# Four slots of one bank for the narrow score rows, and their products issued two steps ahead

## What is computed

```python
b, s, d = x.shape                                  # 2, 1024, 512
qkv = jnp.einsum('bsd,od->bso', x, w_project)
q, k, v = ...                                      # 16 heads of 32
att = jnp.einsum('bhqd,bhkd->bhqk', q, k) / math.sqrt(HEAD_DIM)
att = jnp.where(causal[None, None, :, :], jnp.float32(-1000000000.0), att)
att = jax.nn.softmax(att, axis=-1)
out = jnp.einsum('bhqk,bhkd->bhqd', att, v)
...
h = h + _L0_attn_ref(_layernorm(h, axis=-1), ...)
h = h + _L0_ffn_ref(_layernorm(h, axis=-1), ...)
```

## Time and profile before

| | us |
|---|---|
| median of three runs | 1048.05 (1047.25 to 1049.69) |
| the profiled execution | 1050.3 |
| its span, first to last instruction | 1048.5 |
| TensorE busy | 942.9 (90%) |
| VectorE busy | 667.6 (64%) |
| ScalarE busy | 599.9 (57%) |
| GpSimd busy | 322.1 (31%) |
| mean granted TensorE clock, share of full | 0.964 |

### The profile page before, as it was taken

One profiled execution on the slowest core, in us unless ns is written; L12 is line 12 of the kernel. 1 busy time (PEld: TensorE's weight loads), 2 busy tenths in 40 slices (PEclk: granted clock), 3 DMA queues, 4 the chain that ended last, 5 costly groups with the idle time before them and its releaser, 6 DMA issues.

```text
span 1048.5 us, 21182 instructions
## 1 busy us (share of the span) xinstructions
PE 942.9 (90%) x6811; PEld 687.2 (66%) x6811; DVE 667.6 (64%) x1746; ACT 599.9 (57%) x1304; POOL 322.1 (31%) x320
## 2 busy tenths in 40 slices
PE   6668599999999999999998899899889899989992
PEld 5324458677686868677685687777766566656661
DVE  8885257565666757566676676668756466656660
ACT  7222177677777777776778622211157677766770
POOL 2286120110202020110202036433233575457642
PEclk9689799999999999999999999899889999999997
DMA  6133733260533334150435111431449577747543
GB/s 213 39 97 95 169 82 82 60 134 1 115 79 82 82 72 93 47 131 17 90 77 200 42 71 61 184 148 51 163 151 335 131 135 166 241 83 135 101 71 41
DMA packets 44574, 114.39 MB, mean 109 GB/s; under 512 B 9332, under 2 KB 11380, under 8 KB 42162
## 3 DMA queue, kind: packets, MB, share of 16 engines
q1 hardware_dynamic: 32146, 87.14, 28.2%
q0 software_dynamic: 12320, 25.90, 13.7%
HBM read 53.03 MB, written 25.17 MB: 75 GB/s over the span
## 4 chain that ended last, share of the span: by engine, by line
PE 54%; DMA 20%; issue 9%; DVE 8%; POOL 4%; ACT 3%; POOLq 1%; DVEq 0%; ACTq 0%
DMA out<-xnT,slot_out 20%; PE psum L527 11%; PE psum L497 8%; PE psum L517 7%; PE psum L540 7%; PE psum L502 5%; PE psum L1259 5%; PE psum L1243 3%; PE psum L1341 2%; PE psum L543 2%; POOL hot_all L1479 1%; DVE oh_lo L1554 1%; ACT probsT L594 1%; DVE oh_hi L1552 1%; PE psum L1284 1%
## 5 line engine op out<-in xcount | busy, mean ns | idle before, releaser
L651 DVE CUSTOM_DVE_ANT_0 psum<-psum,mask_row 128x128 f32<-128x128 f32 (+7 forms) x256 | 194.2, 763 | 58.7 <-PE psum L517 56.3
L609 ACT ACTIVATE probs<-psum,nmax 128x128 f32<-128x128 f32 (+7 forms) x256 | 190.7, 745 | 48.2 <-DVE nmax L651 42.4
L527 PE MATMUL psum<-ident,probs 128*128 128x128 f32 x1152 | 172.6, 275 | 4.7 <-ACT probsT L594 3.3
L517 PE MATMUL psum<-k_stack,q_stack 128*128 128x512 f32 (+2 forms) x384 | 154.9, 458 | 18.7 <-ACT probs L609 9.1
L527 PEld LDWEIGHTS psum<-ident,probs 128*128 128x128 f32 x1152 | 136.1, 140 | 37.1 <-issue 18.6
L594 ACT COPY probsT<-psum 128x512 f32<-128x512 f32 (+3 forms) x256 | 129.3, 505 | 37.7 <-PE psum L527 32.9
L497 PE MATMUL psum<-xnT,w_unit 128*128 128x512 f32 x256 | 131.3, 602 | 0.2 <-ACT full L472 0.2
L873 POOL DMA_INDIRECT out<-xnT,slot_out x47 | 94.3, 2005 | 112.5 <-DMA out<-xnT,slot_out 94.5
L444 POOL CAST part_hi<-full 128x512 fp32r<-128x512 f32 x32 | 19.6, 613 | 351.5 <-ACT full L472 246.8
L517 PEld LDWEIGHTS psum<-k_stack,q_stack 128*128 128x128 f32 x384 | 68.5, 201 | 64.0 <-ACT probs L609 41.0
L1392 PE MATMUL psum<-w_dn,gated_T 128*128 x188 | 88.6, 593 | 1.0 <-ACT gated_T L926 1.0
(11 more groups left out here) (238 smaller groups left out, 1845.8 us busy)
## 6 DMA issues: line engine op xcount, KB each, us to landing
w_gu<-in_wgu SPq DMA_DIRECT2D x16, 1024.0 KB, 6.9
q_stack<-part_hi SPq DMA_DIRECT2D x64, 128.0 KB, 2.4
q_stack<-part_lo SPq DMA_DIRECT2D x64, 128.0 KB, 2.4
k_stack<-part_hi SPq DMA_DIRECT2D x64, 128.0 KB, 2.4
k_stack<-part_lo SPq DMA_DIRECT2D x64, 128.0 KB, 2.4
w_dn<-in_wd SPq DMA_DIRECT2D x16, 512.0 KB, 8.8
out<-acc SPq DMA_DIRECT2D x17, 256.0 KB, 2.0
hot_all<-xn SPq DMA_DIRECT2D x4, 1024.0 KB, 8.0
```

What stands on the lines that cost most here:

```text
L517: mm = pe.matmul(dst[:, c0:c1], qs, k_stack[b][:, h, c0:c1], start=True, stop=True)
L527: mm = pe.transpose(bank(4 + m % 2)[:, (j - 4 * k) * P:(j - 4 * k + 1) * P], probs[n % PSLOTS][:, j * P:(j + 1) * P], ident[:, :])
L609: act.activation(probs[n % PSLOTS][:, 0:(i + 1) * P], bank(2 * (n % 2), 2)[:, 0:(i + 1) * P], ACT.Exp, bias=nmax[:, n % 4:n % 4 + 1], scal ...
L651: dve.tensor_tensor_reduce(out=row, in0=row, in1=mask_row[:, (QT - 1 - i) * P:QT * P], scale=1.0, scalar=3.0e38, op0=ALU.add, op1=ALU.min, ...
```

## The change

Steps 0 to 15 get four slots of one bank (`score_bank`: bank n % 4), and steps 16 to 31 keep the two slots of two banks. TensorE issues the narrow score products one step earlier: step n of its loop issues that of n + 2 while this is below 16, the last step of a unit (and the start of the program's attention) issues those of steps 0 and 1 of the next, step 14 issues none, and from step 15 on it is n + 1 as before. The waits follow the slots: a narrow product waits for the exponential of step n - 4 (steps 0 to 3: for those of the unit before that had the banks), step 16 for that of step 13, the last owner of its two banks, and the others as before. VectorE's minimum and ScalarE's exponential read the new place. No instruction is added or removed.

```diff
+        NARROW = STEPS // 2
+
+        def score_bank(n):
+            return bank(n % 4) if n < NARROW else bank(2 * (n % 2), 2)
...
             def scores(u, b, n):
                 i, h = n // GH, n % GH
 
-                pe.wait_ge(s_E, HEAD + u * STEPS + n - 1)
-                dst = bank(2 * (n % 2), 2)
+                if n < 2:
+                    pe.wait_ge(s_E, HEAD + u * STEPS - 1)
+                elif n < 4:
+                    pe.wait_ge(s_E, HEAD + u * STEPS)
+                elif n < NARROW:
+                    pe.wait_ge(s_E, HEAD + u * STEPS + n - 3)
+                elif n == NARROW:
+                    pe.wait_ge(s_E, HEAD + u * STEPS + n - 2)
+                else:
+                    pe.wait_ge(s_E, HEAD + u * STEPS + n - 1)
+                dst = score_bank(n)
...
             def unit(u, b, g, prev, nxt):
 
                 for n in range(STEPS):
-                    if n + 1 < STEPS:
+                    if n + 2 < NARROW:
+                        scores(u, b, n + 2)
+                    elif NARROW <= n + 1 < STEPS:
                         scores(u, b, n + 1)
-                    elif nxt:
+                    elif n + 1 == STEPS and nxt:
                         first_scores(u + 1, 1 - b, g + b)
...
                 scores(u, b, 0)
+                scores(u, b, 1)
...
-                act.activation(probs[n % PSLOTS][:, 0:(i + 1) * P], bank(2 * (n % 2), 2)[:, 0:(i + 1) * P], ACT.Exp,
+                act.activation(probs[n % PSLOTS][:, 0:(i + 1) * P], score_bank(n)[:, 0:(i + 1) * P], ACT.Exp,
...
-                row = bank(2 * (n % 2), 2)[:, 0:(i + 1) * P]
+                row = score_bank(n)[:, 0:(i + 1) * P]
```

## The result

The changed kernel took **1042.76 us**, median of 9 runs (1039.99 to 1048.01), beside 1048.05 for the kernel before in the same comparison; the ratio is 0.9955, 95% interval 0.9935 to 0.9976. The forecast was 1046.7 with a range of 1043.8 to 1049.8, so the time came out faster than the range. Two repeats of the same pair gave 0.9973 (0.9953 to 0.9993) and 0.9969 (0.9951 to 0.9986). Over all three comparisons the changed kernel is 3.8 us faster (difference of the mean times, weighted by their errors), with a standard error of 0.5. Its own median hardly moved (1042.76, 1042.69, 1042.83), while that of the kernel before was 1048.05, 1046.11 and 1046.57: part of the 5.3 us of the first comparison is a kernel before that came out slow in it.

A forecast was written before the change was run, and what follows sets the result against it. TensorE, busy 942.9 of 1048.5 us, was taken as the bound. First unit -0.4, full units +0.1 and last unit -1.1 sum to -1.4 us, giving 1046.7 us against 1048.05, range 1043.8 to 1049.8.

The forecast's parts named there:

- Start of a unit: Score of step 1 goes ahead of the previous unit's eight transposes, so each unit starts 0.12 us later.
- Blocks 0 to 2: Full steps with a projection cannot gain; 1/z comes a score later, moving minimum 12 by 0.12 + 0.23 = 0.35 us.
- Step 13: Slack around steps 12 to 14: transposes of step 13 run at 206.16 instead of 206.14; +0.02 us per full unit.
- (b): Rival, faster: the holes are worth what they look like, 0.34 us in seven units; 1044 us, chance 0.16.
- The hole at step 14: 0.34 us of TensorE stream lost before step 14's score; said to be closed but spent on a later 1/z.
- First unit: Starts at half clock without earlier head sum or eight transposes; -0.4 us, between 0 and -0.5.
- Last unit: No projections; copy of 1/z starts 0.14 us ahead of GpSimd's subtraction, takes 0.23 instead of 1.24: -1.1 us.
- The sum in attention: First unit -0.4, six full units +0.1 and last unit -1.1 give -1.4 us.
- Nothing else moves: Wide half and engine orders unchanged; after 600 us shifts pass through one to one, though TensorE's granted clock may disturb it.
- (a): Rival: last unit's copy of 1/z is caught again, or the wide half gives it back; 1047.9 us, chance 0.28.
- (c): Rival, slower: step 13's margin (needs 0.35, has 0.36 us) is lost, up to 0.35 per unit; 1050.5 us, chance 0.14.

The follow-up runs named there:

- slots alone: The four slots and their waits, but scores issued one step ahead as in the kernel before: 1042.38 us, ratio 0.9955.
- held subtraction: GpSimd's subtraction waits for VectorE's copy of 1/z: kernel before 1046.59 us, 0.9991; changed kernel 1041.74, 0.9967; slots alone 1042.24, 0.9957.
- normalization late: Changed kernel with every normalization moved behind the next step's minimum: 1042.48 us, ratio 0.9969.
- late second score: Changed kernel with the score of step 1 issued behind the eight transposes of step 30, not ahead: 1042.43 us, ratio 0.9974.
- late normalization: Changed kernel with only the normalizations of steps 3, 7 and 11 moved to steps 4, 8 and 12: 1041.06 us, ratio 0.9944.

## Why the prediction was wrong

**Start of a unit, +0.12:** right, +0.12 at the transposes of step 1 and at the first exponential.

**Blocks 0 to 2, minimum 12 at +0.35: the step that failed.** It said that the transpose of 1/z "comes later by that score's width", and added this to the 0.12 of the start. That counts the extra score twice. The order has exactly one score more ahead of any later point, not two: at the start it is a 256-column score, 0.12; at the next blocks it is a wider one in its place, +0.17 and +0.22 in the table above, and 0.21 to 0.24 at minimum 12 in the five units looked at. The shift is 0.23, where 0.35 was forecast. The order of the instructions, which stands ahead of the prediction, shows it; no trace was needed.

**Step 13, +0.02 per unit:** the chain was right in all its links, and with 0.23 put in, its own working gives exponential 13 at 204.94 + 0.23 and the transposes of step 13 at -0.10. The trace has -0.15 at step 13 (its transposes start 0.05 us behind the exponential, where 0.09 was taken), -0.11 at step 14 and -0.10 for the unit. Over six units that is -0.6 us instead of +0.1. The narrow half of the second unit came out at 23.78, outside the 24.00 within 0.1 that the prediction named as its sign, and short of rival (b)'s 23.6. "The hole at step 14 is closed and its time is spent at once on a later 1/z" was two thirds true: of 0.3 us that the hole is worth (slots alone), 0.2 was spent, and, as the held subtraction shows, only because the later 1/z meets a long copy.

**First unit, -0.4:** in the two profiled pairs its length went from 58.62 to 57.89 and from 58.42 to 58.25, and the third had 57.82; about -0.5. The length goes with the moment at which TensorE's granted clock rises to full: 5.8 and 5.4 us behind the first exponential in the kernel before, 4.8, 5.6 and 4.7 in the changed one, and 2.4 to 3.3 in those programs above whose first unit took 56.6 to 56.9. The two executions nearest in this (5.4 and 5.6) differ by 0.17 only. So the sign holds, and how much of the 0.5 is the change is not shown.

**Last unit, -1.1:** right by its mechanism, with some luck in the size. The copy stood 0.07 us ahead of the subtraction, where 0.14 was forecast, and took 0.23; the narrow half is 1.23 shorter (19.51, forecast 19.6). Held apart by a wait, the kernel before gains 0.84 there (19.89), so the GpSimd work in that half was the greater part. The 1.24 us that the sum was built on belong to one execution: in the repeat of the kernel before, the same copy took 0.49, that of block 1 took 0.62 behind a conversion, and the narrow half 20.63. By the rule of the Trainium skill's page "SBUF — State Buffer", section "Who interferes with whom", whoever issues first holds the shared port for its whole instruction. The traces agree: a copy inside which a subtraction starts (558.18, in 558.11 to 558.34) isn't lengthened, and copies issued during a subtraction end only behind it (0.77 us).

**The sum in attention** was -1.4. Against 463.6, the mean of the kernel before's two profiles, the three of the changed kernel stand at -2.4, -2.0 and -2.4. The largest part that was missed is the 0.7 of the full units.

**"Nothing else moves":** wrong, and by more than the double count. The three comparisons give -3.8 us (0.5) in all, of which attention explains -2.25 (461.4, the mean of three, after 463.6). The paragraph named the place of the rest, TensorE's granted clock behind attention, and priced it at nothing. In all three profiles of the changed kernel the 13 products after attention run at full clock (4.53 us); in both of the kernel before the granted clock is 0.72 there (6.13). That is -1.6, and -2.25 - 1.6 = -3.85 meets the measured -3.8. It is not settled that this is more than a fit. The five other programs with 5.86 to 6.14 us there gained what attention gained, within 0.9; but of the four others with 4.53 or 4.54 only one (normalization late) gained 1.5 more than attention, and the late second score and the two with the held subtraction gained 0 to 1.0 less, which is 1.6 to 2.6 less than attention and this 1.6 make together. What sets the clock at that place was not isolated, and the cause of the part behind attention stays open. The remaining 1.5 of the 5.3 us between the first medians came in the first comparison alone.

**Rivals.** (b), holes worth what they look like, 1044 us, was nearest in time, with 0.16 chance. Its mechanism was half right: the Trainium skill's page "Perfetto Trace Analysis", section "Optimization Strategy", says that a repeating gap can mean too few buffers. This case agrees: buffers alone (slots with the old order) brought the 0.3 us of that gap in every full unit. The prediction argued against this with TensorE 23.44 of 24.00 us busy, which leaves 0.56: room enough for it. (a) and (c) didn't come. (c)'s margin at step 13, judged at 0.01 us, was 0.13 by the corrected shift.

## What to carry to other kernels

When an order puts one more instruction of a kind ahead, count at each later point how many stand ahead now and before, and price the difference; don't add up the shifts along the way. Test a change that adds buffers and lead as two changes: the buffers were worth 0.29 us per unit, the second step of lead cost 0.2 of it. Combine the edits too: the two 0.19 us found one at a time (lead, long copy) were one and the same. When an edit moves one instruction, look at what else changed length: the late normalization's 0.36 was in part a copy that had slipped ahead of GpSimd. An engine's idle time names what ended it, not what it is worth: taking away 23 of 56 us of waiting for scores went with 2.5 us, and the kernel that left 52 of them in place was as fast. Moving an instruction out of a critical order in one half of a loop must be looked up in the other half too.

## What the hardware showed

- The copy of 1/z takes 0.23 us alone and up to 1.24 when GpSimd's subtraction is running (0.43, 0.77 and 1.24 in the traces above), always until 0.08 or 0.09 us behind that subtraction's end. A conversion holds it in the same way (0.57 and 0.62). Started 0.02 to 0.12 us ahead of either it took 0.23. Its cost to the time was 0 with the two slots, 0 with four slots and one step of lead, and 0.19 us per full unit with four slots and two steps.
- TensorE, after the same wait of 2.15 us and with the same 13 products, was granted 0.72 to 0.74 of the clock in six programs and 1.00 in five, the same way each time in the two that were repeated, though what they differ in lies in the attention stage alone.
- From the last normalization to GpSimd's last instruction the unchanged code took 436, 445 and 436 us in three profiled executions of one program, and 441.9 and 442.2 in two of the other. Between 600 and 1000 us TensorE spent 14, 24 and 14 us at half clock in the three, in stretches of 3 to 7 us. A single execution tells nothing of 2 us there; attention in the same executions agrees within 0.4.
